# A staged copy of two score groups a unit, a new unit order, and narrower expert tiles in a one-core attention and mixture-of-experts layer

## The reference

```
xn  = layernorm(x)
attention, 16 heads of 16:  softmax((xn Wq^T)(xn Wk^T)^T / 16) (xn Wv^T)
experts: scores = softmax(xn gate_w^T); each token takes the 2 best of 8 by scores + gate_b
  e(xn) = silu((xn w1 + b1) * (xn w3 + b3)) w2 + b2            256 -> 352 -> 256
out = x + attention + sum of the 2 chosen e(xn), weighted by their scores + shared e(xn)
```

## Time and profile before

| | us |
|---|---|
| median of 3 runs (2133.8 to 2136.46) | 2134.87 |
| the profiled execution | 2144.74 |
| its span, first to last instruction | 2142.6 |
| PE / ACT / DVE busy in it | 2117.8 / 2018.4 / 815.0 |

### The profile page before, as it was taken

The page is one execution under the profiler, slowest core; times in us unless marked ns, Lnnn a source line. Parts: engine busy times, 40 slices in busy tenths (PEclk is TensorE's granted clock), DMA queues, the critical chain, the costliest instruction groups (busy, mean ns, idle before and its releaser), DMA issues.

```text
span 2142.6 us, 38345 instructions
## 1 busy us (share of the span) xinstructions
PE 2117.8 (99%) x15758; PEld 979.4 (46%) x15758; DVE 815.0 (38%) x1543; ACT 2018.4 (94%) x2228; POOL 248.6 (12%) x260
## 2 busy tenths in 40 slices
PE   8999999999999999999999999999999999999998
PEld 5734444444444444444444444444444444444442
DVE  7554333333333333333333333333333333344431
ACT  6699999899999999999999999999999999999998
POOL 0305566000000000000000000000000000122230
PEclk9999999999999999999999999999999999999999
DMA  8773333322231313132222232313222221323331
GB/s 284 262 261 96 122 107 95 95 56 71 59 79 47 75 51 85 52 75 62 64 59 71 62 76 55 82 52 70 62 68 71 59 66 58 88 73 104 90 99 32
DMA packets 223310, 187.28 MB, mean 87 GB/s; under 512 B 110623, under 2 KB 192342, under 8 KB 223134
## 3 DMA queue, kind: packets, MB, share of 16 engines
q1 hardware_dynamic: 209454, 148.68, 24.8%
q0 software_dynamic: 12624, 36.08, 5.1%
q10 hardware_dynamic: 1056, 0.07, 0.0%
HBM read 130.21 MB, written 54.53 MB: 86 GB/s over the span
## 4 chain that ended last, share of the span: by engine, by line
PE 95%; ACT 2%; DVE 1%; DMA 1%; POOL 0%; issue 0%; SPq 0%; ACTq 0%; DVEq 0%
PE PS L868 44%; PE PS L855 31%; PE PS L880 12%; PE PS L891 6%; ACT probs L1141 1%; PE PS L674 0%; POOL slot_x L1198 0%; PE PS L687 0%; PE PS L688 0%; PE PS L691 0%; PE PS L756 0%; DMA hones_sb<-in_hones 0%; ACT x_parts L1022 0%; PE PS L663 0%; ACT x_full L1023 0%
## 5 line engine op out<-in xcount | busy, mean ns | idle before, releaser
L1141 ACT ACTIVATE probs<-PS 128x1024 f32<-128x1024 f32 x2048 | 1921.8, 1038 | 81.2 <-PE PS L855 53.8
L868 PE MATMUL PS<-probs,v_head 128*32 128x512 f32 x8192 | 989.1, 600 | 0.9 <-ACT probs L1141 0.8
L855 PE MATMUL PS<-q_ring,k_stack 50*128 50x512 f32 x4096 | 723.8, 441 | 6.8 <-ACT probs L1141 5.5
L855 PEld LDWEIGHTS PS<-q_ring,k_stack 50*128 50x128 f32 x4096 | 331.6, 184 | 598.5 <-ACT probs L1141 541.5
L868 PEld LDWEIGHTS PS<-probs,v_head 128*32 128x32 f32 x8192 | 212.7, 109 | 460.3 <-issue 417.2
L1552 DVE TENSOR_SCALAR gate_in<-PS,bias_sb 128x256 f32<-128x256 f32 x165 | 79.1, 479 | 585.0 <-PE PS L880 584.9
L880 PE MATMUL PS<-x_hi,w_hi 128*128 128x256 f32 (+1 forms) x660 | 202.1, 306 | 3.5 <-DVE x_lo L1605 3.5
L1205 POOL DMA_DIRECT2D slot_y<-y_sb x39 | 27.9, 715 | 1401.8 <-DVE y_sb L1620 1365.5
L880 PE MATMUL PS<-x_hi,w_lo 128*128 128x256 f32 (+1 forms) x660 | 186.3, 282 | 0.0
L880 PE MATMUL PS<-x_lo,w_hi 128*128 128x256 f32 (+1 forms) x660 | 186.0, 282 | 0.0
L880 PEld LDWEIGHTS PS<-x_hi,w_hi 128*128 128x128 f32 (+1 forms) x660 | 118.9, 180 | 50.1 <-issue 50.1
(11 more groups left out here) (171 smaller groups left out, 1163.9 us busy)
## 6 DMA issues: line engine op xcount, KB each, us to landing
w_raw<-in_w SPq DMA_DIRECT2D x110, 352.0 KB
k_stack<-qk_parts SPq DMA_DIRECT2D x120, 128.0 KB
w_raw<-in_w SPq DMA_DIRECT2D x55, 256.0 KB
q_ring<-qk_parts SPq DMA_DIRECT2D x372, 32.0 KB
qk_parts<-part_a SPq DMA_DIRECT2D x20, 512.0 KB, 4.3
slot_x<-zeros SPq DMA_DIRECT2D x39, 256.0 KB, 4.1
slot_in<-slot_x SPq DMA_DIRECT2D x156, 64.0 KB, 2.5
slot_y<-y_sb POOLq DMA_DIRECT2D x39, 256.0 KB, 2.5
```

Source lines behind the costliest of these rows:

```text
L855: last = pe.matmul(bank(2 * score_buffer(turn, g) + r), k_stack[rows, kt * P:(kt + 1) * P], q_ring[rows, sweep, i * QC:(i + 1) * QC], star ...
L868: last = pe.matmul(bank(O_BANK)[VW * j:VW * (j + 1), :], v_head[:, kt, :], probs[:, slot, (j % 2) * QC:(j % 2 + 1) * QC], start=(kt == 0), ...
L1141: nc.scalar.activation(probs[:, prob_slot(g), :], bank(2 * score_buffer(h, g), 2), ACT.Exp, scale=ENERGY_SCALE).then_inc(s_exp, 1)
```

## The change

1. **Staged groups.** In units 2 to 54, VectorE copies the groups at places 3 and 20 of the unit (1024 columns) from their banks into their slot of `probs` (`stage`); ScalarE then takes the exponential in place in SBUF. TensorE may write the banks when the copy is done.
2. **Unit order on TensorE.** S1 up0 S3 V2 S3 up1 S2 V2 S3 V2 S3 V2 S3 down S3 V2 S3 up2 S2 V2 S3 V2 S3 V2 S3 V2 S1, and after the last unit six rounds of S2 V1, down, and S2 V1 to the end. The tanh stands three groups earlier.
3. **A signal per key tile.** Every value step now ends with an increment of `s_vd` (before: 4 of 32 in one sweep, 1 of 32 in the other). ScalarE waits for it ahead of every second exponential.
4. **VectorE's order.** The high part of the next weights is made first in a unit, ahead of the staged copy and the first gate; the low part after `keep`; the down weights at the end; `places` is longer.
5. **Routed tiles.** Full tiles come first, part-filled ones last by size, so that the last seven routed units (40 to 46) need only 224, 192, ... 32 columns (`width`).
6. **Queues.** POOL scatters three tiles a unit in units 1 to 6 and loads the next rows ahead; the last shared tokens come at other places. `load_up` waits for the products only ahead of the biases.

```diff
-TANH_AT = 39
+TANH_AT = 36
+STAGED = (3, 20)
+STAGED_FROM = 2
+SCATTERS = 3
+def width(u):
+    return min(CH, BL * (SZ - u)) if routed(u) else CH
+def staged(g):
+    u, place = divmod(g - FIRST_GROUPS, UNIT_GROUPS)
+    return STAGED_FROM <= u < UNITS and place in STAGED
...
             def load_up(u):
                 sp.wait_ge(s_w13, u)
-                if u >= 2:
-                    sp.wait_ge(s_prod, 3 * (u - 1))
...
+                if u >= 2:
+                    sp.wait_ge(s_prod, 3 * (u - 1))
                 sp.dma_start(bias_sb[:, u % 2, :], ...)
...
-                if kt == NT - 1:
-                    last.then_inc(s_pv, 1)
-                elif sweep == 1 and kt % KTB == KTB - 1:
-                    last.then_inc(s_pvb, 1)
+                last.then_inc(s_vd, 1)
...
-                    if n >= SB:
+                    if n >= SB and staged(n - SB):
+                        pe.wait_ge(s_stage, stages(n - SB))
+                    elif n >= SB:
                         pe.wait_ge(s_exp, n - SB + 1)
...
+                    if n >= NPB and n % 2 == 0:
+                        act.wait_ge(s_vd, (n - NPB) // 2 + 1)
+                    if staged(n):
+                        act.wait_ge(s_stage, stages(n))
+                        scored = probs[:, prob_slot(g), :]
...
-                for v in range(4 * u - 4, min(4 * u, SH)):
+                for v in range(SCATTERS * u, min(SCATTERS * (u + 1), SH)):
...
+            def stage(g):
+                if staged(g):
+                    dve.wait_ge(s_scores, g + 1)
+                    dve.wait_ge(s_vd, (g - NPB) // 2 + 1)
+                    V.tensor_copy(probs[:, prob_slot(g), :], bank(2 * (g % SB), 2)).then_inc(s_stage, 1)
             for u in range(UNITS + 1):
+                if more:
+                    up_hi(u + 1)
+                stage(unit_start(u) + STAGED[0])
                 if real:
                     gate(u, 0)
                     product(u, 0)
...
                 after_values(m + 8)
+                stage(unit_start(u) + STAGED[1])
...
                     keep(u - 1)
+                if more:
+                    up_lo(u + 1)
```

More of the change, by code:

```diff
@@ L97, in unit_start, with stages @@
     return FIRST_GROUPS + u * UNIT_GROUPS
+def staged(g):
+    u, place = divmod(g - FIRST_GROUPS, UNIT_GROUPS)
+    return STAGED_FROM <= u < UNITS and place in STAGED
+def stages(g):
+    return sum(1 for n in range(g + 1) if staged(n))
 def shared_loads(u):
@@ L320, in layer_program @@
         s_vh = sem("s_vh")
-        s_pv = sem("s_pv")
-        s_pvb = sem("s_pvb")
+        s_vd = sem("s_vd")
+        s_stage = sem("s_stage")
         s_osb = sem("s_osb")
@@ L879, in up @@
                     for a, b in ((w13_hi, x_hi), (w13_hi, x_lo), (w13_lo, x_hi)):
-                        last = pe.matmul(f_half(w)[0:FT[j], :], a[u % 2][:, w, dt, j * P:j * P + FT[j]],
-                                         b[:, dt * CH:(dt + 1) * CH], start=(n == 0), stop=(n == 3 * DT - 1))
+                        last = pe.matmul(f_half(w)[0:FT[j], 0:width(u)], a[u % 2][:, w, dt, j * P:j * P + FT[j]],
+                                         b[:, dt * CH:dt * CH + width(u)], start=(n == 0), stop=(n == 3 * DT - 1))
                         n += 1
@@ L887, in down @@
                 n = 0
+                own = min(P, width(u) - t * P)
                 for j in range(3):
@@ L890, in down @@
                     for a, b in ((hid_hi, w2_hi), (hid_hi, w2_lo), (hid_lo, w2_hi)):
-                        last = pe.matmul(f_half(t), a[0:rows, j, t * P:(t + 1) * P], b[0:rows, j, :], start=(n == 0), stop=(n == 8))
+                        last = pe.matmul(f_half(t)[0:own, :], a[0:rows, j, t * P:t * P + own], b[0:rows, j, :], start=(n == 0), stop=(n == 8))
                         n += 1
-                if t == TPU - 1:
+                if (t + 1) * P >= width(u):
                     last.then_inc(s_y, 1)
@@ L914, in down_tile @@
             def down_tile(u, t):
-                if u < 0:
+                if u < 0 or t * P >= width(u):
                     return
@@ L1001, in _ @@
                 next_values(1)
-            for u in range(UNITS + 1):
+            for u in range(UNITS):
                 unit(u)
+            for n in range(6):
+                next_scores(2)
+                next_values(1)
+            down_tile(UNITS - 1, 0)
+            down_tile(UNITS - 1, 1)
             while issued[1] < SWEEPS * NT:
@@ L1228, in _ @@
                 b = c % GB
-                if c % TPC == 0 and shared(SZ + 2 + c // TPC):
-                    load_shared(SZ + 2 + c // TPC)
+                if c in LATE_LOADS:
+                    load_shared(SZ + LATE_LOADS[c])
                 if c >= GB:
@@ L1483, in places @@
             def places():
-                cnt, nt, end, start = (sizes[:, i, :] for i in (0, 1, 2, 4))
+                cnt, full, end, over, start, key, rank, rest, jump = (sizes[:, i, :] for i in range(9))
                 for e in range(E):
@@ L1692, in _ @@
                     keep(u - 1)
+                if more:
+                    up_lo(u + 1)
                 after_values(m + 10)
+                join(u, 2)
+                if routed(u + 1):
+                    turn_tokens(u + 1)
+                if more:
+                    tokens_hi(u + 1)
+                    tokens_lo(u + 1)
+                after_values(m + 12)
+                join(u, 1)
+                after_values(m + 14)
+                if real:
+                    gate(u, 2)
+                    product(u, 2)
+                if u == 0:
+                    places()
+                after_values(m + 16)
                 if real:
@@ L1696, in _ @@
                     down_lo(u)
-                after_values(m + 12)
-                join(u, 1)
-                if routed(u + 1):
-                    turn_tokens(u + 1)
-                if real:
-                    gate(u, 2)
-                    product(u, 2)
-                after_values(m + 14)
-                if more:
-                    tokens_hi(u + 1)
-                    tokens_lo(u + 1)
-                if u == 0:
-                    places()
-                after_values(m + 16)
                 join(u, JOINS - 3)
```

109 lines of the change are left out of this document (64 added, 45 removed).

## The result

The change makes the kernel slower: 2176.46 us (median of 4 runs, 2174.63 to 2177.76) against 2135.66 us (4 runs of before, 2133.8 to 2136.87), ratio 1.0195 (95% interval 1.0183 to 1.0208). I had forecast 2142.6 and a range up to 2162. The sign was right, the size was not: +40.8 us instead of +7.8. The profiled execution took 2174.63 us, span 2172.6.

A forecast was written before the change was run, and what follows sets the result against it. It took TensorE's own work to bound the loop. Terms -12.7 - 6.0 - 6 - 4 + 7.0 + 20.2 + 7.5 + 1.8 = +7.8 us on the median 2134.87 gave 2142.6 us; range 2112 to 2162.

The forecast's parts named there:

- copies and new order: S3 after down, units 2 to 54: staged copies remove one 0.24 us wait of three a unit, -12.7 us.
- unit 7's stop: POOL's queue: three scatters a unit and rows loaded ahead remove the stop at unit 7, -6.0 us.
- narrow tiles: Seven units with fewer columns: shorter up blocks, half of down gone in four, -6 us, bounds 0 and -14.
- tail: After the last unit: S2 V1 gives ScalarE scores evenly, -4 us, bounds 0 and -5.
- units 0 and 1, with the clock there: Unit 0: up1 waits for cast, gate and product, +7.0 us; unit 1: longer `places`, +1.8; lower clock after the stop, 2.5.
- late loads of later units, with the clock: Seven later units: TensorE waits for late up weights, +20.2 us; with lower clock after two stops, +25.2.
- profiled execution against median: Whole kernel: the profiled execution's 9.87 us above the median 2134.87 was assumed to stay the same after the change.
- rival C: Later units: late weights stop nobody, because SP gets through its queue earlier; 2117 us, chance 20%.
- Rival F: Staged copies: another wait takes the place of the one removed; +12.7 us, 2155 us, chance 10%.
- rival B: Runs S3 V2 S3: copies remove all three waits of a unit, another 25.4 us; 2117 us, chance 15%.
- Rival D: Value steps: each of 944 more increments costs TensorE, 9 us per 10 ns; 2167 us at 26.3 ns, chance 5%.
- Rival E: up2 waits in each unit for `keep`, behind a slower second copy; 0.3 us gives +16, 2159 us, chance 10%.

The follow-up runs named there:

- e1: Changed kernel with VectorE's cast of the next up weights put back behind the second product; 2129.72 us, 0.9974 of before.
- e15: Changed kernel, SP putting next-head keys and queries of a unit's last 14 groups (not 4) behind the next up weights; 2167.54 us, 1.0116 of before.
- e17: e14 with POOL issuing gathers one pair at a time, after those of the tile before have landed; 2119.07 us, 0.9929 of before.
- e18: e17 with all of ScalarE's added waits and the table of tiles in its old place; 2130.77 us, 0.9982 of before.
- e5: Changed kernel with the cast back, the unit order of before and no staged copies; 2152.12 us, 1.0063 of before.
- e9: e5 without ScalarE's added waits, the signals kept; 2137.85 us, 0.9997 of before.
- e4: Kernel before with only POOL's part of the change (scatters, row loads, places of late shared tokens); 2133.05 us, 0.9989 of before.
- e10: e1 with only one of ScalarE's added waits a unit, at place 25; 2140.01 us, 1.0015 of before.
- e13: e10 with the table of tiles moved from unit 0 to unit 1; 2150.19 us, 1.0042 of before.
- e14: e13 with the five joins of a unit spread over five places of VectorE's order; 2132.60 us, 0.9956 of before.

## Why the prediction was wrong

The time, step by step. All but the last row are read from first gates of the two profiled executions (that of a unit from 2 on now stands 1.14 us later, behind the copy, which is taken off); the late loads are counted against e1, whose order is the same. The measured rows but the last sum to the 29.9 us between the two executions, to within rounding. The last row is counted from 2134.87, the median that I had.

| step | forecast | measured |
|---|---|---|
| copies and new order | -12.7 | -1 (35.57 to 35.54) |
| unit 7's stop (units 2 to 8) | -6.0 | -7.1 |
| narrow tiles | -6 | -3.5 |
| units 49 to 53 (stops of before, not foreseen) | 0 | -2.6 |
| tail | -4 | -2.2 |
| units 0 and 1, with the clock there | +11.3 | +10.1 |
| late loads of later units, with the clock | +25.2 | +36.1 |
| profiled execution against median | 9.87 long before, and as long after | 1.83 short after: +11.7 |

**Late weights.** The mechanism, most places and the order of size were right (rival C is out by e1 and e15). In unit 0 cast, gate and product stood where I had put them, and TensorE was idle 5.6 us there instead of 7.0. For the later units I count TensorE's stop as the time from up0 to up1, less the same in e1, and give each load's issue against the start of up0:

| load | issue, before | issue, after | forecast stop | measured |
|---|---|---|---|---|
| 22 | 4.2 | 4.4 | 6.7 | 6.6 |
| 54 | 3.4 | 4.1 | 5.9 | 7.4 |
| 20 | 0.7 | 0.8 | 3.2 | 3.0 |
| 15 | -0.3 | 1.6 | 2.2 | 3.7 |
| 47 | -1.4 | 0.7 | 1.1 | 2.7 |
| 52 | -1.6 | -1.2 | 0.9 | 1.3 |
| 13 | -2.3 | -3.3 | 0.2 | 0 |
| 24 | -5.0 | -4.5 | 0 | 1.0 |
| 49 | -8.0 | -8.7 | 0 | 1.2 |
| 53 | -7.9 | -8.7 | 0 | 1.4 |

That is 28.2 us instead of 20.2, and 7.8 us behind the stops instead of 5.0. I had counted two of the later stops there, one of which, at 5.9 us, did not even pass my own "6 us". In the trace five had 1.1 to 2.8 us behind them, those of loads 15, 20, 22, 47 and 54, with a granted clock of 0.50 to 0.73 in the five microseconds after; after the stops of loads 24 and 49 it stood at 1.00. Two steps failed. The first is "the same two views give loads 20, 15, 47, 52 and 13 at 1.09, 2.12, ..." before their gates: I took these distances from the earlier trace rows as they were and did not put them through the new order. SP's last key and query transfers ahead of loads 15 and 47 wait for the group at place 26, and the new order puts up2 ahead of it, so the same group comes later against the next up0. In unit 13, SP's timeline of before, and then of after:

```profile
621.91 0.64 SPq L464 DMA_DIRECT2D k_stack<-qk_parts  x1
...
632.22 0.43 SPq L544 DMA_DIRECT2D w_raw<-in_w  x1
```

```profile
625.83 0.63 SPq L485 DMA_DIRECT2D k_stack<-qk_parts  x1
...
636.11 0.43 SPq L563 DMA_DIRECT2D w_raw<-in_w  x1
```

The next up0 starts on TensorE at 632.55 in the one and at 634.50 in the other:

```profile
632.55 0.39 PE L880 MATMUL PS<-x_hi,w_hi 128*128 128x256 f32 x1
```

```profile
634.50 0.39 PE L898 MATMUL PS<-x_hi,w_hi 128*128 128x256 f32 x1
```

So load 15 comes 0.33 us before up0 in the one and 1.61 after it in the other, 1.9 us later, and load 47 2.1. The others moved by 1.1 us at most, some of them to the earlier side. This step of the prediction is worth some 3 us.

The second is that "all others at least 4.6 before" were left out, with one landing of 4.2 us for every load. For the loads on the list it was well sized: they land 4.1 to 4.7 us after issue, load 54 5.6, load 1 6.9. But the casts behind loads 24, 49 and 53 waited for their transfers until 8.0, 12.1 and 12.3 us after issue, in stretches where I had read no landing. These three stops are 3.6 us, and load 54's later issue and slower landing 1.5. The Trainium skill (DMA: Bandwidth & Descriptors, Anatomy of one DMA) fits 2.0 us plus the bytes at 436 GB/s to transfers on GpSimd's path, which would be an estimate of 3.7 us for 721 KB. These loads are issued by SP, and each of them took longer.

**Copies.** The failed step is "I cost both at nothing", of ScalarE's reads from SBUF and its waits for `s_vd`. The wait behind down did go; 18 waits a unit took the 0.2 us back (e17 and e18, 11.7 us; e5 and e9). With one of them a unit left, the distance is 35.38 (e17), which is 10 of the forecast 12.7 us. An exponential in SBUF takes 1069 ns instead of 1037, for two groups a unit. The reserve "0.03 us per wait would cost 0.5" had the right form; it is 0.06 us at the five places where ScalarE stands ready, nothing elsewhere, and about 0.01 in the mean. Rival F named this outcome, rival B is out, and so is my sentence that TensorE's own work alone bounds the loop: what remains of waits depends on how blocks and S3s follow each other.

**The signals.** Rival D is out: e4, without the added signals, has 35.59, and e9, with them, 35.57. The Trainium skill (TensorE: Matmul & The Clock Gate, The cost: per-tile semaphore tail) puts 26.3 ns on each increment in the tail of a run of matmuls; for 944 that is an estimate of 25 us. Here, with one increment behind 16 matmuls, it is nothing, and the measurement decides. Rival E is out as well: up2 follows its S3 without a wait.

**The base.** "I carry the difference over to the median" failed. It holds only if the profiled execution is long for a reason that the change leaves alone. Some 4 of the 9.87 us (7.1 against 3.2 in units 2 to 7) were stops of that execution, so that I counted them twice: once in the difference and once as -6.0. That -6.0 stands beside a measured -7.1 is therefore no success: both are read from the same execution. The rest is open; medians of before lay between 2134.3 and 2142.6 us in the groups of runs here, so that the execution and the runs that I compared may differ in more than stops.

**Narrow tiles and the tail** had the right sign and were each about half as large as forecast. The -2.6 at units 49 to 53 goes with POOL's part, which alone (e4) has no stop there. In e9, without the added waits, the narrow units are 4.6 us shorter in all, in e1 3.5.

## What to carry to other kernels

An operation that waits for a transfer belongs behind everything that the pacing engine wants next; moving it ahead cost 47 us here. When an order changes, put each queue that waits for a count of it through the new order before using old distances, and do not price every landing by the one that was easy to read. A buffer copy takes a wait away only where the next block gives the slower engine time to catch up; elsewhere the wait moves on. And a stop seen in one profiled execution needs a second one before it becomes a term.

## What I had not expected of the hardware

A wait that holds nothing back still costs ScalarE 0.06 us where it stands ready for its scores, and nothing where it has work in hand; that made 0.17 to 0.25 us a unit. Signals in TensorE's last matmul of a value step cost nothing (1024 of them). The same 704 KB landed 4.3 us after issue in one unit and 12.3 in another. TensorE's stops of 0.9 to 3.9 us in units 49 to 53 of e10, e13 and e14 fall into bursts of six to ten gathers of POOL, and one pair at a time, with the joins spread, left none; but e1 has such a burst and no stop. What happens inside such a stop is open.
